# A two-layer vision transformer kernel: first-layer softmax divided as rows, merged second-layer products, unrolled loops and a new order of work

## The reference

```
h = h + L0_attn(layernorm(h))      # q, k, v without bias, rotation, causal softmax, Wo
h = h + L0_ffn(layernorm(h))       # 8 experts, top 2: sum of gate_e * (x @ w_in[e].T) @ w_out[e].T
h = h + L1_attn(layernorm(h))      # below
h = h + L1_ffn(layernorm(h))       # ternary weights, gelu, layernorm of 1024, ternary projection

# L0_attn
scores = where(causal, -inf, einsum("bhtd,bhsd->bhts", q, k) * scale)
out = einsum("bhts,bhsd->bhtd", softmax(scores), v)

# L1_attn: xn = ln(x, g1, b1)
q, k = lin(xn, Wq, bq) / sqrt(16), lin(xn, Wk, bk);   v = lin(xn, Wv, bv) as 8 sets of 16
out = einsum("bhij,bjrd->bihrd", softmax(q k), v)
comp = softmax over the 8 sets of concat([lin(xn, Wqv, bqv) / sqrt(32), out]) @ Ws.T + bs
out = x + lin((comp * out).sum(sets), Wf, bf)
return out + lin(relu(lin(ln(out, g2, b2), Wr1, br1)), Wr2, br2)
```

## Time and profile before

| | us |
|---|---|
| median of the runs | 561.5 |
| profiled execution | 560.32 |
| its span, first to last instruction | 558.5 |
| TensorE (PE) busy | 506.9 (91%) |
| VectorE (DVE) busy | 375.7 (67%) |
| ScalarE (ACT) busy | 272.9 (49%) |
| GpSimd (POOL) busy | 190.3 (34%) |
| mean granted TensorE clock | 0.977 |

### The profile page before, as it was taken

How to read it: one execution, slowest core, us unless ns; L and a number is a source line. 1 busy time by engine, 2 the same in 40 slices (tenths; PEclk the granted TensorE clock), 3 DMA queues, 4 the chain that set the end, 5 groups by cost and what they waited for, 6 DMA issues and landing times.

```text
span 558.5 us, 12004 instructions
## 1 busy us (share of the span) xinstructions
PE 506.9 (91%) x3850; PEld 424.5 (76%) x3850; DVE 375.7 (67%) x943; ACT 272.9 (49%) x634; POOL 190.3 (34%) x257
## 2 busy tenths in 40 slices
PE   2969999999999887789999999999999989889996
PEld 2758878878787665567778888888888778668885
DVE  4554464555466667565997878878878787648874
ACT  3021213232331363547668777777777886434332
POOL 3320321322323311375463364364363311222230
PEclk9788899999999999999999999999999999979999
DMA  8741333243140500000000000000000000000000
GB/s 318 285 175 38 141 150 120 80 175 150 31 169 0 179 2 2 0 1 2 1 1 2 2 0 0 0 0 0 0 0 0 2 0 1 2 9 21 21 18 22
DMA packets 8685, 29.60 MB, mean 53 GB/s; under 512 B 1936, under 2 KB 3152, under 8 KB 6352
## 3 DMA queue, kind: packets, MB, share of 16 engines
q1 hardware_dynamic: 8656, 29.23, 14.4%
HBM read 27.98 MB, written 1.25 MB: 52 GB/s over the span
## 4 chain that ended last, share of the span: by engine, by line
PE 42%; DVE 5%; issue 5%; ACT 3%; POOL 1%; DVEq 1%; POOLq 0%; ACTq 0%
PE score L2051 6%; PE tb L1803 3%; PE score L1868 3%; PE bz L2081 3%; PE tb L1805 3%; PE tb L1804 3%; PE bank L1805 3%; PE bank L1804 3%; PE bank L1803 3%; PE tb L1886 2%; PE bz L2063 2%; PE bz L1817 2%; PE bz L1803 1%; DVE we_h L1433 1%; PE tb L1817 1%
## 5 line engine op out<-in xcount | busy, mean ns | idle before, releaser
L378 POOL TENSOR_TENSOR h<-h,scaled 114x256 f32 (+1 forms) x88 | 69.0, 784 | 49.3 <-ACT scaled L681 42.7
L330 POOL TENSOR_TENSOR small<-small,half 114x1 f32<-114x1 f32 x44 | 25.7, 584 | 139.4 <-DVE small L964 139.3
L547 ACT ACTIVATE p_exp<-sc,cst 114x608 f32<-114x608 f32 x66 | 48.1, 794 | 24.7 <-DVE sc L1045 24.7
L1915 PE MATMUL bz<-ebuf 128*128 128x256 f32 x256 | 58.9, 383 | 0.0
L1915 PEld LDWEIGHTS bz<-ebuf 128*128 128x128 f32 x256 | 47.8, 192 | 6.0 <-issue 0.2
L1886 PE MATMUL tb<-cst,p_exp 114*114 114x114 f32 x352 | 44.0, 266 | 9.0 <-ACT p_exp L547 3.4
L555 ACT ACTIVATE pt<-tb 114x456 f32<-114x456 f32 x66 | 34.6, 556 | 35.3 <-PE tb L1886 35.3
L2051 PE MATMUL score<-v,pt 114*114 114x137 f32 x352 | 48.9, 282 | 0.3 <-ACT o L648 0.3
L1886 PEld LDWEIGHTS tb<-cst,p_exp 114*114 114x114 f32 x352 | 35.2, 134 | 18.2 <-ACT pt L555 6.7
L681 ACT ACTIVATE scaled<-bank,gl 114x256 f32<-114x256 f32 x88 | 39.0, 473 | 17.3 <-DVE gl L1249 5.9
L2051 PEld LDWEIGHTS score<-v,pt 114*114 114x114 f32 x352 | 44.1, 178 | 2.1 <-issue 0.4
(11 more groups left out here) (216 smaller groups left out, 1338.7 us busy)
## 6 DMA issues: line engine op xcount, KB each, us to landing
ebuf<-in_w_in SPq DMA_DIRECT2D x8, 1024.0 KB, 4.8
ebuf<-in_w_out SPq DMA_DIRECT2D x8, 1024.0 KB, 6.8
x_raw<-in_x_tiles SPq DMA_DIRECT2D x11, 342.0 KB, 3.0
out<-h SPq DMA_DIRECT2D x10, 114.0 KB
raw<-in_w_a SPq DMA_DIRECT2D x4, 256.0 KB, 4.2
ebuf<-in_fc SPq DMA_DIRECT2D x1, 1024.0 KB, 5.6
ebuf<-in_proj SPq DMA_DIRECT2D x1, 1024.0 KB, 7.6
raw<-in_w_a SPq DMA_DIRECT2D x2, 384.0 KB, 5.2
```

Source lines behind the costliest of these rows:

```text
L378: gp.tensor_tensor(h[0:R, t, :], h[0:R, t, :], scaled[0:R, e % 4, :], ALU.add).then_inc(moe_acc, 1)
L547: act.activation(p_exp[0:R, :, b * S:(b + 1) * S], sc[0:R], ACT.Exp, bias=cst[0:R, CB + b:CB + b + 1], scale=SCALE).then_inc(exps, 1)
L1915: last = pe.matmul(bz[:, m * D:(m + 1) * D], ebuf[:, 0, c * D + m * P:c * D + (m + 1) * P], ebuf[:, 1, c * D:(c + 1) * D], start=(c == 0), ...
```

## The change

What it does, part by part:

- The exp is written once, densely, in place (`a2_exp`). VectorE sums its rows, inverts the sums and multiplies (`a2_norm`, three operations). ScalarE writes three scaled copies into `p_exp` (`a2_wide`), the scale being 1 inside an image and 0 outside (`inside`, made once). The products with `hsum` are gone, and so are `a2_recip` and the `a2_o` of VectorE; rounding and rest are taken straight from PSUM. `scores` waits for `oT_lo` instead of `o_ready`.
- In `wc` a row of weights is now q (256), v and its scores (136), k (256), query scores (16): W4 = 664. `c2_qk` makes the first WQ = 392 columns into bank `tb1`, `c2_v` the other 272 into `tb0`, directly after. `c2_rows` copies two pieces of 256. `c2_qT` waits for both pieces and for `v1_ready` at 2t + 2, because it overwrites the bank that `c2_v` of VectorE reads; `c2_kT` for 2t + 1. The load of these weights is four transfers instead of one.
- The gate's high x high and high x low products are one of 16 columns; VectorE adds the two halves when it copies.
- In the head, `a1_x(1)`, patch product 1 and the products of tile 1 come sooner; `prep_products` goes behind `a1_k(1)`, and `prep_qv`, patch product 2 stand ahead of `combine(1, 1)`. In `a_step` the first half of `combine(t, 1)` goes ahead of the transposes.
- The loops `c_step` and `d_step` are written out on all engines, and the whole order from tile 7 on is new: steps of the last feed-forward stand between the last tiles of the second layer's attention.

The core of the diff:

```diff
+            def a2_exp(n):
+                act.wait_ge(shifted, 2 * n + 2)
+                act.activation(sc[0:R], sc[0:R], ACT.Exp, scale=SCALE).then_inc(dense, 1)
+
+            def a2_wide(n, batches=range(G)):
+                act.wait_ge(scaled_rows, n + 1)
+                since(act, pt_mm, 4 * n)
+                for b in batches:
+                    act.activation(p_exp[0:R, :, b * S:(b + 1) * S], sc[0:R], ACT.Copy,
+                                   scale=inside[0:R, b:b + 1]).then_inc(exps, 1)
...
-            def a2_recip(t):
-                dve.wait_ge(pv0_mm, t + 1)
-                V.reciprocal(rinv0, score[:, 0, 2 * R:4 * R]).then_inc(rinv0_ready, 1)
-
-            def a2_o(t):
-                dve.wait_ge(rinv0_ready, t + 1)
-                since(dve, oT_lo, t)
-                V.tensor_tensor(y2[:], two(score[:, 0, 0:2 * R]), two(rinv0), ALU.mult).then_inc(o_ready, 1)
+            def a2_norm(n, k):
+                if k == 0:
+                    dve.wait_ge(dense, n + 1)
+                    V.tensor_reduce(psum_rows[0:R, 0], sc[0:R], AX, ALU.add).then_inc(summed, 1)
+                elif k == 1:
+                    dve.wait_ge(summed, n + 1)
+                    V.reciprocal(psum_rows[0:R, 1], psum_rows[0:R, 0]).then_inc(inverted, 1)
+                else:
+                    dve.wait_ge(inverted, n + 1)
+                    V.tensor_tensor(sc[0:R], sc[0:R], psum_rows[0:R, 1].unsqueeze(2).broadcast_to([R, H, S]),
+                                    ALU.mult).then_inc(scaled_rows, 1)
...
             def c2_qk(t):
                 pe.wait_ge(t2["lo"], t + 1)
-                product(tb[1][0:R, :], xth[1], xtl[1], wc, C_QK, 2 * D, (0, 2 * D)).then_inc(qk1_mm, 1)
+                since(pe, pt_odd, 2 * (t + T))
+                product(tb[1][0:R, 0:WQ], xth[1], xtl[1], wc, C_QK, W4, (0, WQ)).then_inc(qk1_mm, 1)
 
             def c2_v(t):
-                pe.wait_ge(q_ready, 2 * (t + T) + 2)
-                product(tb[0][0:R, 2 * R:2 * R + W2], xth[1], xtl[1], wc, C_V, W2, (0, W2)).then_inc(v1_mm, 1)
+                pe.wait_ge(t2["lo"], t + 1)
+                product(tb[0][0:R, 0:D + H], xth[1], xtl[1], wc, C_QK, W4, (WQ, W4)).then_inc(v1_mm, 1)
 
             def c2_qT(t):
-                pe.wait_ge(qk1_out, t + 1)
+                pe.wait_ge(qk1_out, 2 * t + 2)
+                pe.wait_ge(v1_ready, 2 * t + 2)
                 turned(tb[0][:, 0:2 * R], qk_rows[:, 0:D]).then_inc(qkT1_mm, 1)
...
             def a_step(t):
...
                 a1_v(t)
+                combine(t, 1, (0, 1, 2, 3))
                 a1_turn(t - 1)
-                combine(t, 1)
+                combine(t, 1, (4, 5, 6, 7))
...
+            a1_x(1)
             a1_turn(0)
-            a1_x(1)
-            a2_pv(0)
             a1_qk(1)
             a1_v(1)
+            a2_pv(0)
             combine(1, 0)
             a1_qT(1)
             a1_kT(1)
-            combine(1, 1)
-            a1_patch(2)
-            prep_qv()
             pe.wait_ge(wa_lo, 6)
             a2_wo(0)
+            prep_qv()
+            a1_patch(2)
+            combine(1, 1)
             pe.wait_ge(prep, 5)
```

More of the change, by code:

```diff
@@ L417, in d2_bias @@
                 gp.tensor_tensor(h[0:R, t, :], h[0:R, t, :], bw[0:R], ALU.add).then_inc(hb_ready, 1)
[L419 to L425, removed]
             split_wc(8)
             split_x(9)
+            split_x(10)
             a1_rope(8)
-            split_x(10)
             rstd(nA, 9)
@@ L570, in _ @@
             a1_x(0)
+            act.activation(inside[0:R], cst[0:R, CB:CB + G], ACT.Exp).then_inc(init, 1)
             a1_v(0)
@@ new lines, in _ @@
+            c3_stats(1)
+            gate(5, 0)
+            plus_eps(n1, 6)
+            aggr(n4, 1)
+            mix(2, 0)
+            plus_eps(n4, 1)
+            gate(5, 1)
+            gate(5, 2)
+            gate(5, 3)
+            mix(2, 1)
+            gate(5, 4)
+            mix(2, 2)
+            c3_normed(1)
+            c2_v(3, (0, 1))
+            mix(2, 3)
+            gate(5, 5)
+            mix(2, 4)
+            c2_k(3, (0, 1))
+            gate(5, 6)
+            gate(5, 7)
+            gate(5, 8)
@@ new lines, in _ @@
+            mix(2, 12)
+            gate(6, 0)
+            c3_res(1)
+            c2_x(4)
+            gate(6, 1)
+            c1_normed(7)
+            gate(6, 2)
+            gate(6, 3)
+            gate(6, 4)
+            c3_sum(2)
+            c3_stats(2)
+            gate(6, 5)
+            aggr(n4, 2)
+            normed1(4)
+            c2_v(4, (0,))
+            gate(6, 6)
+            gate(6, 7)
+            plus_eps(n4, 2)
+            c1_stats(8)
+            mix(3, 0)
+            c2_v(4, (1,))
@@ new lines, in _ @@
+            mix(3, 9)
+            normed2(5)
+            c1_x(7)
+            mix(3, 10)
+            normed1(5)
+            mix(3, 11)
+            gate(7, 0)
+            gate(7, 1)
+            mix(3, 12)
+            c3_res(2)
+            gate(7, 2)
+            c2_x(5)
+            plus_eps(n1, 8)
+            gate(7, 3)
+            c3_sum(3)
+            gate(7, 4)
+            c3_stats(3)
+            c1_normed(8)
+            aggr(n4, 3)
+            c1_stats(9)
+            plus_eps(n4, 3)
@@ new lines, in _ @@
+            softmax_sub(5 + T, (0, 1))
+            c2_eps(6, (0,))
+            mix(4, 5)
+            mix(4, 6)
+            mix(4, 7)
+            mix(4, 8)
+            mix(4, 9)
+            c2_eps(6, (1,))
+            mix(4, 10)
+            mix(4, 11)
+            normed2(6)
+            c1_x(8)
+            mix(4, 12)
+            c3_res(3)
+            c1_normed(9)
+            gate(8, 0)
+            gate(8, 1)
+            c2_x(6)
+            gate(8, 2)
+            gate(8, 3)
+            gate(8, 4)
@@ new lines, in _ @@
+            c2_x(7)
+            gate(9, 4)
+            plus_eps(n1, 10)
+            aggr(nD, 0)
+            c3_res(4)
+            gate(9, 5)
+            mix(6, 0)
+            mix(6, 1)
+            gate(9, 6)
+            c2_v(7, (0,))
+            gate(9, 7)
+            c2_v(7, (1,))
+            mix(6, 2)
+            c2_k(7, (0,))
+            gate(9, 8)
+            c2_k(7, (1,))
+            mix(6, 3)
+            mix(6, 4)
+            c2_stats(8)
+            mix(6, 5)
+            c3_sum(5)
```

1819 lines of the change are left out of this document (1205 added, 614 removed).

## The result

| | us |
|---|---|
| before, median of 4 runs | 561.4 (556.8 to 562.3) |
| after, median of 4 runs | 599.5 (594.0 to 601.2) |
| ratio, 95% interval | 1.068 (1.059 to 1.077) |
| span of the profiled execution, before and after | 558.5 and 596.8 |
| TensorE busy, before and after | 506.9 (91%) and 511.9 (86%) |

The account below looks back on a forecast made before the run. TensorE was taken as the bound; head +3.8, loop -5.0 and -1.2, first layer's end +3.0, second layer -4.4 and +1.0, end -6.1 and -2.3 sum to -11.2: 549.1 us, 550.3 as a median, range 541 to 560.

Parts of the forecast that it names:

- head, to the first combination of the loop: Head: combination 1 ends later, so expert 2's weights land later and the clock falls; +3.8 us, bounds 0 and +6.
- loop, to scores(7): First layer's loop: sums by ones go, expert's DMA limits a step's gain to 1.0; -5.0 and -1.2 us.
- tiles 7 to 10: Behind the first layer's loop: longer softmax without a combination to hide behind; +3.0 us, bounds -1 and +6.
- second layer: Second layer's 11 tiles: merged products and gate -4.4 us, turned queries' new wait for VectorE's additions +1.0.
- end: After the second layer's loop: interleaved order removes idle time, -6.1 us, and low clock, -2.3; bounds -12 and 0.
- rival B: End: interleaving brings little, idle only moves because VectorE is busy there; 557.8 us, chance 0.20.
- a doubt about the multiply: Head: the softmax multiply might lose up to 1.6 us beside a GpSimd split, by the shared port rule.
- Rival C: Second layer: turned queries wait for operations ahead of VectorE's additions, 1.8 us a tile; 565.7 us, chance 0.09.
- rival D: Every tile: the longer softmax costs its added 2.8 us instead of being hidden; 569.9 us, chance 0.04.

Follow-up runs that it names:

- out_beside_centre: tern_and_head with `d2_out(t)` right behind `d2_centre(t)` on VectorE for tiles 3, 4 and 6 to 10; 567.7 us, 1.014 to the kernel before.
- gelu_behind_mix: tern_and_head with the first half of `d1_gelu(1)` on ScalarE moved behind `c2_mix(10)` and `d2_hi(0)`; 571.3 us, 1.024 to the kernel before.
- end_filled: rows_in_loop_only with one feed-forward step put between the steps of c3(10) at the end; 544.2 us, 0.971 to the kernel before.
- new_operations_old_order: Changed kernel's operations and unrolling in the order of the kernel before, the first layer's loop as changed; 596.0 us, 1.064 to the kernel before.
- rows_in_loop_and_gate: rows_in_loop_only with the gate in four products and the adding copy; 546.3 us, 0.974 to the kernel before.
- tern_and_head: Changed kernel with `tern_sum(0)` moved right ahead of `tern_sum(1)` and `combine(1, 1)` right behind `a1_kT(1)`; 577.7 us, 1.032 to the kernel before.
- rows_in_loop_only: Kernel before, second-half loops unrolled, plus row division in tiles 0 to 6, changed head with combination ahead of `prep_qv`, split second combination; 547.2 us, 0.978.
- rows_in_every_tile: rows_in_loop_only with tiles 7 to 10 divided as rows too; 566.2 us, 1.011 to the kernel before.

## Why the prediction was wrong

The prediction's steps against the two traces (after minus before, us):

| step of the prediction | predicted | measured | off by |
|---|---|---|---|
| head, to the first combination of the loop | +3.8 | +6.0 | 2.2 |
| loop, to scores(7) | -6.2 | -1.3 | 4.9 |
| tiles 7 to 10 | +3.0 | +20.0 | 17.0 |
| second layer | -3.4 | +3.5 | 6.9 |
| end | -8.4 | +10.1 | 18.5 |
| sum | -11.2 | +38.3 | 49.5 |

- **The end** is the step that failed most. The prediction took two thirds of the idle time away because the order was more interleaved, and looked at no call of it: -6.1 us of idle time and -2.3 for the clock were given, and from `c2_x(10)` on TensorE's idle time rose from 13.1 to 20.4 us and its clock fell from 0.96 to 0.94. It named against itself (rival B) that VectorE's list is full there. Walked through, the new order puts `d2_out(t)` behind the next tile's low halves, so that output step, the next output product and the next centring form one chain from tile to tile (9.8 us of waits; out_beside_centre takes back 6.7 us), and it puts exponentials between Gelus (gelu_behind_mix, 4.5 us). The two were not run together. Interleaving as such was not the fault: end_filled wins 2.7 to 4.9 us by it, in the one chain where TensorE waited.
- **Tiles 7 to 10** hold an omission and a size that was off. The omission: `tern_sum(0)`, moved ahead of `a1_x(8)`, is a moved step with a DMA behind it, and was not looked at; 10 us. The size: the added chain was right (2.8 predicted; scores to transposes 8.9 instead of 6.2 in tile 9, though 10.8 in tile 10, multiply 0.81 for 0.8, sum 0.79). But the clock was taken as unchanged: from the transposes to the value products 3.3 to 3.6 us were given and 5.7 measured, at the lower level, and 2.7 instead of 2.0 from there to the next scores. With the sum moved, the stretch still costs 9.9 us for the 3.0 given; the upper bound was 6. (The head, too, had a doubt about the multiply, up to 1.6 us lost beside a GpSimd operation: there it took 0.97 us, in the ten other tiles 0.79.)
- **The second layer**: the merged products gave what was said (1.9 us for the 392 and 272 columns, in new_operations_old_order, where the 512 and 152 took 2.2; the gate 0.33 for 0.53). The failed step is that TensorE's work was taken as the bound because its busy share was 100%. Of the step 6.2 us are the softmax of VectorE and ScalarE; savings inside that piece give nothing (rows_in_loop_and_gate), and what was moved ahead of the scores came out as 1.6 us a step (new_operations_old_order). Rival C had the right place, at 0.64 us a tile in the old order, but not the cause: not operations ahead of the additions, but the value products of the tile before. In the changed order it is six waits of at most 0.6, and the loss lies in uneven steps of 19.6 to 22.4 us; which call makes each of them long was not tried.
- **The head** went as reasoned, `combine(1, 1)` late behind `prep_qv`, and cost 6.0 for 3.8 (upper bound 6). The term that was too small is the end of combination 1: 60.3, not 57 (bounds 55 to 59.5), with the clock at 0.50 from 49.3 to 56.2 already, over the small products (3.5 us for the 1.84 counted) and the patch product ahead of it. The weights landed 7.5 us later, as said. **The loop**: the reasoning held, with the expert's DMA as the bound and 18.95 for 18.7; but expert 3's weights were late as well, so the first step took 22.6 us, where a step of the kernel before takes 19.7. The prediction let the late load and the low clock end with the head. Where the combination stands ahead (tern_and_head, rows_in_loop_only) the loop takes 5.3 and 5.0 us less than before, for the 6.2 given.
- The softmax in the loop is hidden, as predicted; rival D did not happen there.

## What to carry to other kernels

Where every engine has a list written by hand, predict from the list: for each call that moves, ask what it waits for and who stands behind it, above all for a call that waits for a DMA. A TensorE without a gap need not be the bound; look whether the distance between a product and the product that needs its result over other engines is the same in every step, and count only work outside that piece. A wait is named for the last engine of a chain: ask what that engine itself waited for (ScalarE's DMA behind the first loop, TensorE's own value products ahead of the turned queries). A longer chain is free where other work covers it (the loop) and costs its length and the low clock where it does not, so choose the form by place: here rows in the loop, the ones product behind it.

## What the hardware showed that was not expected

- Gaps cost nearly twice here. In rows_in_every_tile the clock is 0.81 over 82 us, with 11.6 us of waits for `p_exp` in four places, the longest 4.4; busy time grew by 8.4 us on less work. In rows_in_loop_only, with waits of at most 1.7 us in the same stretch, the clock stayed at 1.00.
- A rolled loop cost 0.38 us a step in the `d` loop (6.07 us) and nothing in the `c` loop (20.95 us).
- The dense exp without a bias operand takes 710 ns where the wide one with a bias takes 794, for the same 608 columns. The wide one also writes a tile with gaps; which of the two makes the difference no run separates.
- Beside a GpSimd subtraction from 32.31 to 34.36 us, a normalisation on VectorE that began at 32.80 ended at 34.51, 1.71 us instead of the usual 0.52.
